# Two steps at a time in the loops of a staged attention on one Trainium2 core

## The chip, the core and the metric

The kernel runs on one core of one Trainium2 chip. The time is the device time of one execution in microseconds (us). The engines work side by side, each on an instruction list of its own, and meet only at semaphores: TensorE (PE in the profile, its weight loads are PEld), ScalarE (ACT), VectorE (DVE), GpSimd (POOL) and SyncE (SP), which here only starts transfers.

## What is computed

x is 2 batches of 1024 rows of 128 numbers. Four attentions, two linear layers and two mixtures of experts follow each other, each behind a layer norm and added to x. All attentions have 16 heads of 64 and work on 1024 queries and 1024 keys of a batch:

```python
# a0: keys and values shared by all heads, no mask
sim  = einsum('bnhk,bmk->bnhm', q, k) / sqrt(64)
o    = einsum('bnhm,bmv->bnhv', softmax(sim), v)
out  = einsum('bnhv,dhv->bnd', o, output_proj)
# a1 (own keys and values for each head), a2 (latent keys and values, shared), a3 (as a1, with biases)
masked = where(causal, -inf, einsum('bhsq,bhtq->bhst', q, k))
out    = einsum('bhst,bhtv->bhsv', softmax(masked / sqrt(dq)), v)   # then the output projection
```

## The kernel before

One program of phases runs in this order: setup, norm, a0, norm, a1, norm, a2, norm, experts, norm, a3, norm, experts, final. A phase ends with a barrier of all engines. The change is in `attention_phase`, which serves a0 to a3.

**Items and steps.** A pair of heads of one batch is an item; there are 16 items. Within an item, half s of the queries (512 each) meets blocks k of 128 keys; one such meeting is a step. Without a mask (a0) an item has NS = 16 steps. With a mask it has NS = 12: four for the first half of the queries (k = 0 to 3, all on the diagonal, of 512, 384, 256 and 128 queries) and eight for the second (k = 0 to 3 of 512 queries each, k = 4 to 7 on the diagonal of 512, 384, 256, 128). Steps of all items are numbered through by g.

**What a step is on TensorE.** Round g of the loop issues four things:

- `scores(g)` (L506, L509, L514): keys by queries of both heads, two matmuls of 64 rows that lie side by side in the upper and the lower half of the array (64*128 in the profile), then minus the row maximum (L509) and, on the diagonal, the mask (L514). The result goes to one of two score buffers of two banks.
- `chunk(g + LEAD)`, LEAD = 10 (L530, L535): the same scores in a faster type, queries by up to 512 keys, also 64*128, ten steps ahead, for their row maxima only. It has one buffer of two banks, `chunk_ps`, so each chunk waits until VectorE has taken the maxima of the one before:

```python
def chunk(c):
    if c >= 1:
        pe.wait_ge(maxed, c)
```

- `mix_step(g - LAG)`, LAG = 2 (L549): probabilities by values. The two heads lie side by side in the columns of the array (128*64), and all steps of a half add up in bank 6.
- the small matmuls that the table `when` puts at this round (`use_small`): the projections `q` and `k` (L560) and `v` (L565), `top`, which transposes the row maxima (L570), `total`, the sums of the probabilities (L574, 128*64), and `out`, the output projection (L578). All but `total` use the whole array (128*128). All of them write bank 7, and each waits until the one before has been copied out:

```python
def use_small(n, kind, i, part):
    if n >= 1:
        pe.wait_ge(small_out, n)
```

**The others.** ScalarE takes exponentials (`exps`, L609), copies the finished product out of bank 6 (`take_mixed`, L617) and all small results but `out` out of bank 7 (`take_small`, L631 to L650). VectorE takes the maxima of a chunk (`row_max`, L680; L687 joins two halves), inverts the sums in four quarters (`invert`, L700), multiplies (`normalise`, L708) and adds `out` (`add_out`, L713). GpSimd adds up probabilities (`add_up`, L765) and rounds q and k (L755). Every engine's list follows the same loop over g, written out when the program is built. In an item of the masked attentions, by step number within the item, `q` stands at 9 and 0, `out` at 1 and 10, `top` at 2 and 6, `total` at 3 and 7, and in a1 and a3 also `v` at 4 and 5, `k` at 8 and 11. In a0 (of 16) `q` stands at 1 and 4, `out` at 2 and 10, `total` at 3 and 11, `top` at 6 and 14. Inversions stand at the four steps behind a `total`, the normalisation at the fifth.

Of the kernel before, what the change touches and what calls it, by code (L numbers as in the profile page):

```python
# [43 lines left out]
LEAD = 10  # L44
LAG = 2
# [337 lines left out]
def attention_phase(nc, m, a, tag, dram, after, causal, biased=False, shared=False):  # L383
# [5 lines left out]
    with phase(nc) as (ctx, new_sem):  # L389
# [33 lines left out]
        def step(g):  # L423
            i, j = divmod(g, NS)
            s, k = steps[j]
            return i, s, k, max(0, k - s * TPG) * P if causal else 0
# [28 lines left out]
            uses_at.setdefault(g, []).append((n, kind, i, part))  # L455
        FIRST = uses[0][0]
        LAST = uses[-1][0] + 1

        rounds = [(kind, i, part) for _, kind, i, part in uses if kind in "qk"]
        round_of = {one: n for n, one in enumerate(rounds)}  # L460
# [35 lines left out]
        def _(pe):  # L496
            def scores(g):
                i, s, k, lo = step(g)
                if g >= 2:
                    pe.wait_ge(exped, g - 1)  # L500
                if g == first_step(i, s):
                    pe.wait_ge(small_out, use_of["top", i, s] + 1)
                out, width = score[g % 2], BANK - lo
                diagonal = causal and k >= s * TPG
                for head, rows in enumerate(HEADS):
                    nc.tensor.matmul(out[:, head, 0:width], a.k[rows, key_slot(i, 3), k * P:(k + 1) * P],  # L506
                                     a.q[rows, i % 3, s * BANK + lo:(s + 1) * BANK], start=True, stop=False)
                for head, rows in enumerate(HEADS):
                    last = nc.tensor.matmul(out[:, head, 0:width], a.pick[rows, :], a.max_row[rows, s, lo:BANK],  # L509
                                            start=False, stop=not diagonal)  # L510
                if diagonal:
                    for half in range(2):
                        for head, rows in enumerate(HEADS):
                            last = nc.tensor.matmul(out[:, head, half * HD:(half + 1) * HD], a.causal[rows, half, :],  # L514
                                                    a.shifted_ident[rows, 0, 0:HD], start=False, stop=half == 1)
                last.then_inc(scored, 1)
# [64 lines left out]
            if biased:  # L581
# [3 lines left out]
                                            stop=n == PAIRS - 1)  # L585
                last.then_inc(bias_mm, 1)
                pe.wait_ge(bias_out, 1)
            for g in range(FIRST, LAST):
                if 0 <= g < TOTAL:
                    scores(g)  # L590
                if 0 <= g + LEAD < TOTAL:
                    chunk(g + LEAD)
                if 0 <= g - LAG < TOTAL:
                    mix_step(g - LAG)
                for use in uses_at.get(g, ()):
                    use_small(*use)

        @block.scalar
        def _(act):
            def exps(g):  # L600
                i, s, k, lo = step(g)
                act.wait_ge(scored, g + 1)
                if k > 0 and ring_slot[g] >= RING:
                    before = step_of_ring[ring_slot[g] - RING]
                    act.wait_ge(weighed, before + 1)
                    act.wait_ge(summed, sums_done[before])
                elif k == 0 and i > 0:
                    act.wait_ge(small_mm, use_of["total", i - 1, s] + 1)
                act.activation(probabilities(g)[:, :, lo:BANK], score[g % 2][:, :, 0:BANK - lo], ACT.Exp)\  # L609
                    .then_inc(exped, 1)  # L610

            def take_mixed(i, s):
                u = unit(i, s)
                act.wait_ge(weighed, end_step(i, s))
                if u >= 2:
                    act.wait_ge(normed, u - 1)
                act.activation(a.mixed_raw[:, u % 2, :], mix, ACT.Copy).then_inc(mixed_out, 1)  # L617

            def take_small(n, kind, i, part):
                act.wait_ge(small_mm, n + 1)  # L620
                if kind in "qk":
                    if i >= 3 and not (shared and kind == "k"):
                        act.wait_ge(scored, (i - 2) * NS)
                    slot = key_slot(i, 3) if kind == "k" else i % 3
                    dst = (a.k if kind == "k" else a.q)[:, slot, part * BANK:(part + 1) * BANK]
                    scale = SCALE if kind == "q" else 1.0
                    if biased:
                        at = 1 if kind == "k" else 0
                        if n == 0:
                            act.wait_ge(bias_scaled, 1)  # L630
                        last = act.activation(dst, small, ACT.Identity, bias=a.qk_bias[:, i // B, at:at + 1],  # L631
                                              scale=scale)
                    else:
                        last = act.activation(dst, small, ACT.Copy, scale=scale)  # L634
                elif kind == "v":
                    if shared:
                        last = act.activation(a.v[:, i, :, 0:HD], small.rearrange("p (t c) -> p t c", c=HD), ACT.Copy)
                    else:
                        if i >= 2:
                            act.wait_ge(weighed, (i - 1) * NS)  # L640
                        last = act.activation(a.v[:, i % 2, part * TPG:(part + 1) * TPG, :],
                                              small.rearrange("p (t c) -> p t c", c=P), ACT.Copy)
                elif kind == "top":
                    if i >= 1:
                        act.wait_ge(scored, end_step(i - 1, part))
                    last = act.activation(a.max_row[:, part, :], small, ACT.Copy)  # L646
                else:
                    if unit(i, part) >= 1:
                        act.wait_ge(inverted, QUARTERS * unit(i, part))
                    last = act.activation(a.total[:], small, ACT.Copy)  # L650
                last.then_inc(small_out, 1)

            for g in range(FIRST, LAST):
                if 0 <= g < TOTAL:
                    exps(g)
                if 0 <= g - LAG < TOTAL:
                    i, s, _, _ = step(g - LAG)
                    if g - LAG + 1 == end_step(i, s):
                        take_mixed(i, s)
                for n, kind, i, part in uses_at.get(g, ()):  # L660
                    if kind != "out":
                        take_small(n, kind, i, part)

        @block.vector
        def _(dve):
# [61 lines left out]
            for i in range(ITEMS):  # L727
                for s in range(2):
# [1 line left out]
                    for quarter in range(QUARTERS):  # L730
                        inverts_at[at + quarter] = (i, s, quarter)
                    norms_at[at + QUARTERS] = (i, s)
            for g in range(FIRST, LAST):
                if 0 <= g + LEAD < TOTAL:
                    row_max(g + LEAD)
                if g in norms_at:
                    normalise(*norms_at[g])
                if g in inverts_at:
                    invert(*inverts_at[g])
                for n, kind, i, part in uses_at.get(g, ()):  # L740
                    if kind == "out":
                        add_out(n, i, part)

        @block.gpsimd
        def _(pool):
            def round_off(n, kind, i, part):
                pool.wait_ge(small_out, n + 1)
                if i >= 2 and not (shared and kind == "k"):
                    pool.wait_ge(chunked, (i - 1) * NS)
                cols = slice(part * BANK, (part + 1) * BANK)  # L750
                if kind == "k":
                    src, dst = a.k[:, key_slot(i, 3), cols], a.k_near[:, key_slot(i, 2), cols]
                else:
                    src, dst = a.q[:, i % 3, cols], a.q_near[:, i % 2, cols]
                pool.tensor_copy(dst, src).then_inc(rounded, 1)  # L755

            def add_up(g):
                i, s, k, lo = step(g)
                pool.wait_ge(exped, g + 1)
                if k == 1:  # L760
                    pool.wait_ge(weighed, g)
                else:
                    pool.wait_ge(summed, sums_done[g] - 1)
                sums = a.sums[:, unit(i, s) % 2, :, lo:BANK]
                pool.tensor_tensor(sums, sums, probabilities(g)[:, :, lo:BANK], ALU.add).then_inc(summed, 1)  # L765

            for g in range(FIRST, LAST):
                if 0 <= g - 1 < TOTAL and step(g - 1)[2] > 0:
                    add_up(g - 1)
                for n, kind, i, part in uses_at.get(g, ()):  # L770
                    if kind in "qk":
                        round_off(n, kind, i, part)
# [308 lines left out]
```

## Time and profile before

| | us |
|---|---|
| time, median of 3 runs | 3050.87 (3048.06 to 3052.62) |
| time of the profiled execution | 3052.27 |
| its span, first to last instruction | 3050.4 |
| TensorE busy | 2823.4 (93%) |
| VectorE busy | 1749.3 (57%) |
| GpSimd busy | 1479.3 (48%) |
| ScalarE busy | 1196.1 (39%) |

The profile takes one execution; busy time is a mean over phases with different limits. In a row of TensorE the start is when the instruction began and the duration runs to the moment when its last column has left the array, so rows of matmuls that follow each other overlap: what one costs is read from its start to the start of the next.

### The profile page before, as it was taken

The numbers are of one execution on the slowest core, as the hardware profiler recorded it, in microseconds if no ns is written. First come the engines' busy times: TensorE is split into PE (matmuls) and PEld (weight loads), VectorE is DVE, ScalarE is ACT, GpSimd is POOL, SyncE is SP. The second block draws the span as 40 slices with busy tenths as digits, with TensorE's granted clock in tenths as the row PEclk, the third lists the DMA queues.
The fourth block names the chain that finished last, engine by engine and source line by source line (L and its number), as shares of the span: only waits on it lengthen the run. The fifth ranks groups of instructions, "written<-read, shape, count | busy, mean of one in ns | idle before, by whom it ended". The sixth has DMA issues, their size and how long they took to land. (4 is left out here: it accounts for less than half of the span.)

```text
span 3050.4 us, 41067 instructions
## 1 busy us (share of the span) xinstructions
PE 2823.4 (93%) x16065; PEld 1207.0 (40%) x16065; DVE 1749.3 (57%) x2337; ACT 1196.1 (39%) x1607; POOL 1479.3 (48%) x932
## 2 busy tenths in 40 slices
PE   4999999999949999999948999999787999999978
PEld 3333333333324444444423444444333444444433
DVE  2566666666573555555573666666543555555653
ACT  2344444444413444444412444444222444444422
POOL 1576677766703555555502555555301555555520
PEclk9999999999958999999956999999897999999979
DMA  4000000000000000000001000000000000000000
GB/s 101 1 1 1 1 1 1 1 1 1 1 1 16 1 1 1 1 1 1 1 0 28 1 1 1 1 1 1 1 0 1 1 1 1 1 1 1 1 1 14
DMA packets 21345, 14.63 MB, mean 5 GB/s; under 512 B 3233, under 2 KB 20001, under 8 KB 21026
## 3 DMA queue, kind: packets, MB, share of 16 engines
q1 hardware_dynamic: 21154, 12.01, 1.6%
q8 instruction: 128, 2.10, 0.3%
q14 instruction: 63, 0.52, 0.1%
HBM read 9.91 MB, written 2.10 MB: 4 GB/s over the span
## 5 line engine op out<-in xcount | busy, mean ns | idle before, releaser
L765 POOL TENSOR_TENSOR sums<-sums,p 128x1024 f32<-128x1024 f32 (+3 forms) x704 | 1352.0, 1920 | 696.6 <-PE ps L549 626.4
L680 DVE TENSOR_REDUCE half_max<-ps 128x2 f32<-128x1024 f32 (+3 forms) x640 | 703.4, 1099 | 665.0 <-PE ps L530 537.5
L609 ACT ACTIVATE p<-ps 128x1024 f32<-128x1024 f32 (+3 forms) x704 | 597.6, 849 | 666.8 <-PE ps L509 384.1
L506 PE MATMUL ps<-q,k 64*128 64x512 f32 (+3 forms) x3328 | 819.0, 569 | 0.0
L549 PE MATMUL ps<-p,v 128*64 128x512 f32 (+3 forms) x2816 | 635.0, 530 | 0.0
L509 PE MATMUL ps<-max_row,pick 64*128 64x512 f32 (+3 forms) x1664 | 572.2, 681 | 0.0
L700 DVE RECIPROCAL inverse<-total 128x128 f32<-128x128 f32 x512 | 478.8, 940 | 51.2 <-ACT total L650 40.8
L506 PEld LDWEIGHTS ps<-q,k 64*128 64x128 f32 x3328 | 251.3, 185 | 509.0 <-issue 340.4
L530 PE MATMUL ps<-k_near,q_near 64*128 64x512 f32 (+2 forms) x1664 | 340.7, 403 | 27.9 <-DVE half_max L680 21.4
L680 DVE TENSOR_REDUCE neg_max<-ps 128x2 f32<-128x256 f32 x192 | 158.5, 826 | 331.0 <-PE ps L535 330.7
L755 POOL CAST k_near<-k 128x512 fp32r<-128x512 f32 x72 | 44.0, 611 | 464.4 <-ACT k L634 261.7
L530 PEld LDWEIGHTS ps<-k_near,q_near 64*128 64x128 f32 x1664 | 164.1, 191 | 153.1 <-issue 107.5
L509 PEld LDWEIGHTS ps<-max_row,pick 64*128 64x128 f32 x1664 | 161.7, 188 | 143.6 <-issue 129.0
L755 POOL CAST q_near<-q 128x512 fp32r<-128x512 f32 x128 | 78.2, 611 | 287.7 <-ACT q L634 242.7
L549 PEld LDWEIGHTS ps<-p,v 128*64 128x64 f32 x2816 | 139.9, 134 | 156.5 <-issue 122.5
L609 ACT ACTIVATE sums<-ps 128x1024 f32<-128x1024 f32 x128 | 131.0, 1023 | 145.4 <-PE ps L509 85.0
L578 PE MATMUL ps<-mixed,o_w 128*128 128x512 f32 x256 | 147.7, 659 | 24.3 <-DVE mixed L708 24.3
L560 PE MATMUL ps<-xn_t,q_w 128*128 128x512 f32 x256 | 154.3, 686 | 5.7 <-ACT k L634 2.7
L650 ACT ACTIVATE total<-ps 128x512 f32<-128x512 f32 x128 | 76.4, 597 | 169.7 <-PE ps L574 169.7
L549 PE MATMUL ps<-sums,v 128*64 128x512 f32 x512 | 138.1, 617 | 0.1
L574 PE MATMUL ps<-sums,ones 128*64 128x512 f32 x512 | 132.6, 596 | 4.1 <-DVE y_t L713 2.3
L646 ACT ACTIVATE max_row<-ps 128x512 fp32r<-128x512 f32 x128 | 76.4, 597 | 151.2 <-PE ps L570 151.2
(138 smaller groups left out, 2067.4 us busy)
## 6 DMA issues: line engine op xcount, KB each, us to landing
q_w<-in_wq SPq DMA_DIRECT2D x3, 512.0 KB
o_w<-in_wo SPq DMA_DIRECT2D x3, 512.0 KB
k_w<-in_wk SPq DMA_DIRECT2D x2, 512.0 KB
v_w<-in_wv SPq DMA_DIRECT2D x2, 512.0 KB
out<-x SPq DMA_DIRECT2D x4, 256.0 KB, 2.8
scratch<-in_wq_t SPq DMA_DIRECT2D x1, 512.0 KB, 5.1
scratch<-in_w_out SPq DMA_DIRECT2D x1, 512.0 KB, 7.2
wq_latent<-scratch SPq DMA_DIRECT2D x1, 512.0 KB, 3.3
```

The source lines that it names most:

```text
L506: nc.tensor.matmul(out[:, head, 0:width], a.k[rows, key_slot(i, 3), k * P:(k + 1) * P], a.q[rows, i % 3, s * BANK + lo:(s + 1) * BANK], st ...
L509: last = nc.tensor.matmul(out[:, head, 0:width], a.pick[rows, :], a.max_row[rows, s, lo:BANK], start=False, stop=not diagonal)
L530: last = nc.tensor.matmul(chunk_ps[:, head, 0:hi - lo], a.q_near[rows, i % 2, t * P:(t + 1) * P], a.k_near[rows, key_slot(i, 2), lo:hi], s ...
L549: last = nc.tensor.matmul(mix[rows, lo:BANK], a.v[:, key_slot(i, 2), k, value_columns(head)], probabilities(g)[:, head, lo:BANK], start=k ...
L560: last = nc.tensor.matmul(small, weights, m.xn_t[:, at:at + BANK], start=True, stop=True)
L574: last = nc.tensor.matmul(small[rows, :], a.ones[:], a.sums[:, unit(i, part) % 2, head, :], start=True, stop=True)
L578: last = nc.tensor.matmul(small, w.o[:, i // B, :], a.mixed[:], start=True, stop=True)
L609: act.activation(probabilities(g)[:, :, lo:BANK], score[g % 2][:, :, 0:BANK - lo], ACT.Exp)\
L680: last = v.tensor_reduce(out, chunk_ps[:, :, 0:hi - lo], AX.X, ALU.max, negate=True)
L700: v.reciprocal(a.inverse[:, cols], a.total[:, cols]).then_inc(inverted, 1)
L755: pool.tensor_copy(dst, src).then_inc(rounded, 1)
L765: pool.tensor_tensor(sums, sums, probabilities(g)[:, :, lo:BANK], ALU.add).then_inc(summed, 1)
```

## The change

On TensorE, ScalarE and VectorE the loop takes two steps, g and g + 1 with g even: first scores (or exponentials, or maxima) of both, then both products (or what belongs to them), then the small matmuls of both (or their copies, or additions). GpSimd's order stays. No instruction and no wait is added or removed.

```diff
+        PAIRS_OF_STEPS = [(g, g + 1) for g in range(FIRST - FIRST % 2, LAST, 2)]
...
-            for g in range(FIRST, LAST):
-                if 0 <= g < TOTAL:
-                    scores(g)
-                if 0 <= g + LEAD < TOTAL:
-                    chunk(g + LEAD)
-                if 0 <= g - LAG < TOTAL:
-                    mix_step(g - LAG)
-                for use in uses_at.get(g, ()):
-                    use_small(*use)
+            for pair in PAIRS_OF_STEPS:
+                for g in pair:
+                    if 0 <= g < TOTAL:
+                        scores(g)
+                    if 0 <= g + LEAD < TOTAL:
+                        chunk(g + LEAD)
+                for g in pair:
+                    if 0 <= g - LAG < TOTAL:
+                        mix_step(g - LAG)
+                for g in pair:
+                    for use in uses_at.get(g, ()):
+                        use_small(*use)
...
+                for g in pair:
+                    if 0 <= g + LEAD < TOTAL:
+                        row_max(g + LEAD)
+                for g in pair:
+                    if g in norms_at:
+                        normalise(*norms_at[g])
+                    if g in inverts_at:
+                        invert(*inverts_at[g])
+                for g in pair:
+                    for n, kind, i, part in uses_at.get(g, ()):
+                        if kind == "out":
+                            add_out(n, i, part)
```

ScalarE's loop is changed in the same way: `exps` of both, `take_mixed`, `take_small` of both.

TensorE in a1, steps 6 and 7 of an item, before (a name left of the arrow is written, names right of it are read; x2 and x4 count equal matmuls):

```order
L506 MATMUL ps<-q,k 128x512 x2
L509 MATMUL ps<-max_row,pick 128x512 x2
L530 MATMUL ps<-k_near,q_near 128x512 x2
L549 MATMUL ps<-sums,v 64x512 x2
L570 MATMUL ps<-ident,neg_max 128x128 x4
L506 MATMUL ps<-q,k 128x512 x2
L509 MATMUL ps<-max_row,pick 128x512 x2
L530 MATMUL ps<-k_near,q_near 128x128 x2
L535 MATMUL ps<-causal,shifted_ident 128x128 x4
L549 MATMUL ps<-p,v 64x512 x2
L574 MATMUL ps<-sums,ones 64x512 x2
```

The same two steps after the change, where lines of TensorE's code are one higher:

```order
L507 MATMUL ps<-q,k 128x512 x2
L510 MATMUL ps<-max_row,pick 128x512 x2
L531 MATMUL ps<-k_near,q_near 128x512 x2
L507 MATMUL ps<-q,k 128x512 x2
L510 MATMUL ps<-max_row,pick 128x512 x2
L531 MATMUL ps<-k_near,q_near 128x128 x2
L536 MATMUL ps<-causal,shifted_ident 128x128 x4
L550 MATMUL ps<-sums,v 64x512 x2
L550 MATMUL ps<-p,v 64x512 x2
L571 MATMUL ps<-ident,neg_max 128x128 x4
L575 MATMUL ps<-sums,ones 64x512 x2
```

Both pairs of scores and chunk now stand ahead of both products, and `total` (L575) stands straight behind `top` (L571), where two scores, a chunk and a product stood between them.

VectorE in a1, steps 10 and 11, before:

```order
L680 TENSOR_REDUCE half_max<-ps 128x2
L700 RECIPROCAL inverse<-total 128x128
L680 TENSOR_REDUCE half_max<-ps 128x2
L700 RECIPROCAL inverse<-total 128x128
L713 TENSOR_TENSOR y_t<-y_t,ps 128x512
```

After, where L680 is L687, L700 is L707 and L713 is L720:

```order
L687 TENSOR_REDUCE half_max<-ps 128x2 x2
L707 RECIPROCAL inverse<-total 128x128 x2
L720 TENSOR_TENSOR y_t<-y_t,ps 128x512
```

The second maximum has moved ahead of an inversion and of the addition of `out`, and the addition now stands behind both inversions.

## Rows read from the trace of the kernel before

**Rows 1.** The page, busy time of the engines.

```profile
PE 2823.4 (93%) x16065; PEld 1207.0 (40%) x16065; DVE 1749.3 (57%) x2337; ACT 1196.1 (39%) x1607; POOL 1479.3 (48%) x932
```

**Rows 2.** Windows, a steady item of a0 and of a1: stretch, length, each engine's busy us, clock.

```profile
200.00:247.66 47.66, 47.66 (x220) 16.78 (x216) 29.92 (x31) 21.15 (x24) 34.23 (x17) 1.00 0.00 1
1200.00:1237.58 37.58, 37.58 (x258) 16.85 (x254) 21.77 (x25) 16.75 (x25) 19.36 (x14) 1.00 0.01 1
```

**Rows 3.** Timeline of TensorE in a0: start, us, engine, line, operation, names, form, count.

```profile
402.13 1.08 PE L549 MATMUL ps<-sums,v 128*64 128x512 f32 x4
403.14 1.12 PE L578 MATMUL ps<-mixed,o_w 128*128 128x512 f32 x2
404.20 1.13 PE L506 MATMUL ps<-q,k 64*128 64x512 f32 x4
...
405.73 1.08 PE L549 MATMUL ps<-p,v 128*64 128x512 f32 x4
406.63 1.03 PE L574 MATMUL ps<-sums,ones 128*64 128x512 f32 x4
407.59 0.70 PE L506 MATMUL ps<-q,k 64*128 64x512 f32 x2
```

**Rows 4.** Timeline of TensorE, start of a1: chunks that waited; in brackets idle time before.

```profile
942.16 0.49 PE L530 MATMUL ps<-k_near,q_near 64*128 64x512 f32 x2
943.98 0.45 PE L530 MATMUL ps<-k_near,q_near 64*128 64x384 f32 x2 [1.32 <-DVE half_max L680]
...
944.48 0.70 PE L560 MATMUL ps<-xn_t,k_w 128*128 128x512 f32 x1
...
951.20 0.33 PE L530 MATMUL ps<-k_near,q_near 64*128 64x128 f32 x2 [0.64 <-DVE half_max L680]
...
951.58 0.65 PE L549 MATMUL ps<-sums,v 128*64 128x512 f32 x2
```

**Rows 5.** The same start of a1, VectorE.

```profile
942.70 1.23 DVE L680 TENSOR_REDUCE half_max<-ps 128x2 f32<-128x1024 f32 x1 [1.62 <-PE ps L530]
```

**Rows 6.** Groups by line and form, VectorE's maxima: busy us, mean ns, idle before.

```profile
L680 DVE TENSOR_REDUCE half_max<-ps 128x2 f32<-128x1024 f32 x496 | 605.1, 1220 | 599.8 <-PE ps L530 537.5 <-PE ps L535 62.0
...
L680 DVE TENSOR_REDUCE neg_max<-ps 128x2 f32<-128x768 f32 x48 | 46.0, 959 | 115.4 <-PE ps L535 115.4
L680 DVE TENSOR_REDUCE neg_max<-ps 128x2 f32<-128x256 f32 x48 | 20.4, 426 | 61.3 <-PE ps L535 61.0
```

**Rows 7.** Timeline of TensorE, steady a1: steps 11, 2 (its transposes) and 3.

```profile
1202.54 0.49 PE L506 MATMUL ps<-q,k 64*128 64x128 f32 x4
...
1203.49 0.54 PE L549 MATMUL ps<-p,v 128*64 128x384 f32 x2
...
1213.73 0.66 PE L570 MATMUL ps<-ident,neg_max 128*128 128x128 f32 x4
1214.32 0.49 PE L506 MATMUL ps<-q,k 64*128 64x128 f32 x4
...
1215.20 0.54 PE L549 MATMUL ps<-p,v 128*64 128x384 f32 x2
```

**Rows 8.** Timeline of TensorE, end of a3: two small matmuls in a row.

```profile
2928.76 1.10 PE L578 MATMUL ps<-mixed,o_w 128*128 128x512 f32 x2 [1.53 <-DVE mixed L708]
2930.63 1.08 PE L574 MATMUL ps<-sums,ones 128*64 128x512 f32 x4 [0.78 <-DVE y_t L713]
```

**Rows 9.** The same end of a3, VectorE.

```profile
2929.89 0.69 DVE L713 TENSOR_TENSOR y_t<-y_t,ps 128x512 f32<-128x512 f32 x1 [1.28 <-PE ps L578]
```

**Rows 10.** Groups by line and form: an inversion, ScalarE's copy of `total`.

```profile
L700 DVE RECIPROCAL inverse<-total 128x128 f32<-128x128 f32 x512 | 478.8, 940 | 51.2 <-ACT total L650 40.8
...
L650 ACT ACTIVATE total<-ps 128x512 f32<-128x512 f32 x128 | 76.4, 597 | 169.7 <-PE ps L574 169.7
```

**Rows 11.** Windows at the start of a3: as rows 2; 1.00 or 0.50 is the clock.

```profile
2331.20:2334.60 3.40, 2.18 (x16) 1.19 (x14) 2.16 (x3) 0.60 (x1) 0.00 (x0) 1.00 0.00 0
2334.60:2338.00 3.40, 3.37 (x10) 0.95 (x8) 1.40 (x2) 0.69 (x1) 0.61 (x1) 0.50 0.00 0
```

More of the change, by code:

```diff
@@ L651, in take_small @@
                 last.then_inc(small_out, 1)
[L653 to L662, printed above, removed]
+            for pair in PAIRS_OF_STEPS:
+                for g in pair:
+                    if 0 <= g < TOTAL:
+                        exps(g)
+                for g in pair:
+                    if 0 <= g - LAG < TOTAL:
+                        i, s, _, _ = step(g - LAG)
+                        if g - LAG + 1 == end_step(i, s):
+                            take_mixed(i, s)
+                for g in pair:
+                    for n, kind, i, part in uses_at.get(g, ()):
+                        if kind != "out":
+                            take_small(n, kind, i, part)
         @block.vector
@@ L732, in _ @@
                     norms_at[at + QUARTERS] = (i, s)
[L733 to L742, printed above, removed]
+            for pair in PAIRS_OF_STEPS:
+                for g in pair:
+                    if 0 <= g + LEAD < TOTAL:
+                        row_max(g + LEAD)
+                for g in pair:
+                    if g in norms_at:
+                        normalise(*norms_at[g])
+                    if g in inverts_at:
+                        invert(*inverts_at[g])
+                for g in pair:
+                    for n, kind, i, part in uses_at.get(g, ()):
+                        if kind == "out":
+                            add_out(n, i, part)
         @block.gpsimd
@@ L765, in add_up @@
                 pool.tensor_tensor(sums, sums, probabilities(g)[:, :, lo:BANK], ALU.add).then_inc(summed, 1)
-            for g in range(FIRST, LAST):
+            for g in range(PAIRS_OF_STEPS[0][0], PAIRS_OF_STEPS[-1][-1] + 1):
                 if 0 <= g - 1 < TOTAL and step(g - 1)[2] > 0:
```

## The prediction, made before the changed kernel was run

> **What bounds the kernel now.** First the page: TensorE is busy 93% of the span, the next engine 57% [rows 1]. That share is a mean, so then windows over one steady item: 47.66 us in a0 and 37.58 in a1, TensorE busy in all of them, no gap, clock 1.00 [rows 2]; The 16 items of these two make 763 and 601 us; a2 and a3 go through the same code as a1. In the attentions, then, whatever lengthens TensorE's list lengthens the kernel, and everything else is hidden. So the question is what each piece costs from its start to the next start, and which waits of TensorE are satisfied only because other work stands between.
>
> **What the change can save.** Before, TensorE goes scores, product, small, scores. A product between two pieces of another shape takes 1.01 us (402.13 to 403.14); followed by `total`, which has the product's shape (128*64), 0.90 (405.73 to 406.63) [rows 3]. Leaving a shape thus costs 0.11; `total` itself leaves the shape but does not enter it and takes 0.96 (406.63 to 407.59), so the bare work of such matmuls is 0.85, and entering a shape costs 0.05. Two products in a row save 0.16 a pair; where one of them had `total` behind it, which now stands behind `top` or `out`, only 0.05. Scores behind a chunk save a similar amount, below. The Trainium skill, "TensorEngine Tiling (Array Packing)", Key Properties, says that a change of tiling mode drains TensorE. The trace agrees, at 0.11 for the drain, and by this rule alone the kernel gets faster (rival 2).
>
> **Wait 1: the second chunk.** Chunk c + 1 waits for the maxima of chunk c. Before, the next scores, a product and perhaps a small matmul covered them; now only `scores(g + 1)` does. The start of a1 shows the wait bare: chunk at 942.16 ends 942.65, maxima 942.70 to 943.93, next chunk 943.98 [rows 4, 5], so 0.05 on either side. Maxima take 1.22, 0.96 and 0.43 us for chunks of 512, 384 and 128 keys [rows 6]. A chunk's end lies 0.07 behind the start of the next piece (403.21 against 403.14) [rows 3]. Behind a wait a chunk takes 0.50 with 384 keys and mask, 0.38 with 128 [rows 4], so 0.56 and 0.44 for 512 and 256, and 0.42 for 512 without mask (0.49 less 0.07) [rows 4]. Hence the second scores and chunk of a pair now take 0.17 + maxima + chunk instead of their length of before.
>
> - a0: before 1.53 (404.20 to 405.73) [rows 3]; now 0.17 + 1.22 + 0.42 = 1.81. +0.28 a pair, 8 pairs: +2.2 an item.
> - Masked: before, the six odd steps take 1.54, 0.88, 1.65, 1.48, 1.42, 0.95, together 7.92 (step 11 from 1202.54 to 1203.49, step 3 from 1214.32 to 1215.20; two of the six) [rows 7]. Now 6 x 0.17 = 1.02, maxima of the first chunks 4 x 1.22 + 0.96 + 0.43 = 6.27, second chunks 2 x 0.56 + 2 x 0.44 + 0.38 + 0.50 = 2.88: 10.17. +2.25 an item. The worst pair is steps 10 and 11, whose second scores are 128 wide: +0.94.
>
> This contains what the missing change of shape saves. Products give back 6 x 0.16 + 2 x 0.05 = 1.06 in a0, 4 x 0.16 + 2 x 0.05 = 0.74 in a masked item.
>
> **Wait 2: two small matmuls in one pair.** Both write bank 7, and the second waits until ScalarE or VectorE has copied out the first. Before, scores, a chunk and a product stood between, 0.88 us for scores and chunk alone at the narrowest pair (step 3) [rows 7]. Now nothing does. By the table, one item has such doubles at steps (2,3) and (10,11) in a0; (0,1), (2,3), (6,7) in a2; at all six pairs in a1 and a3. The end of a3 shows one: `out` starts 2928.76, ends after 1.10, VectorE adds 0.69 from 2929.89, `total` starts 2930.63, so 1.87 start to start [rows 8, 9]; without the wait it is 1.06 (403.14 to 404.20) [rows 3]. The follower costs 1.08 instead of 1.03 [rows 3, 8], so 0.05 more. With ScalarE's copy (0.60) [rows 10]:
>
> - 512-column matmuls: 1.12 + 0.05 + 0.60 + 0.05 = 1.82, then 1.11; before 2 x 1.06. +0.81.
> - `top`, `total`: transposes end after 0.66 (before they took 0.59, 1213.73 to 1214.32) [rows 7]: 0.66 + 0.70 + 1.01 against 0.59 + 0.96. +0.82.
> - `out`, `total` in a0: 1.87 + 1.01 against 2.02. +0.86.
> - `out`, `k` (steps 10 and 11): VectorE first has the second maxima, 0.96, and two inversions of 0.94 [rows 6, 10], together some 2.8 us behind the chunk; the matmul ends at about 2.7, so it costs 0.1 more. +0.95.
>
> Sums an item: a0 1.7, a2 2.45, a1 5 x 0.82 + 0.95 = 5.05, a3 the same (its copies add a bias, which I take to cost nothing).
>
> **VectorE later.** Both maxima now stand ahead of inversions, normalisation and addition. Behind the second maxima, 1.27 us after the chunk, two inversions are done at 3.1. In a0 the next chunk ends no earlier than 1.86 + 1.53 = 3.39: covered, by 0.3. In a1 and a3 small matmuls cover it. In a2 steps 2 to 5 have no small matmul between: two narrow products (0.8) and scores (1.53) end at 2.3, so maxima start 0.7 late: +0.7 an item there. If cover in a0 is gone too, four pairs lose up to 0.3 each, +20 us in all; from below it is nothing. ScalarE and GpSimd have time: 21.15 and 34.23 of 47.66 us [rows 2].
>
> **The sum.** a0: 2.2 - 1.06 + 1.7 = 2.9; a1 and a3: 2.25 - 0.74 + 5.05 = 6.55; a2: 2.25 - 0.74 + 2.45 + 0.7 = 4.7. Times 16 items: 46 + 105 + 105 + 75 = 331. The first item of each attention has uses ahead of step 0 that already stood bare, about half an item of each: 10 less, 321. The profiled execution took 3052.3, with a span of 3050.4, and becomes 3373; it lies 1.4 above the median of the runs, so 3372 by the median. **Forecast 3373.**
>
> **Rivals.**
>
> 1. *The clock falls.* At the start of a3 a stretch of 3.4 us with TensorE busy 2.18 was followed by one at clock 0.50 [rows 11]. The new order puts up to two waits of nearly 1 us close together (steps 0 and 1: maxima, then `q`, `out`), with busy shares by the profile's count near two thirds. Against it: the rest of each item is dense, and by the terms above TensorE waits in under a fifth of it. If each of 48 masked items lost one such stretch, half of 3.4 us, it costs 48 x 1.7 = 82: **3455**; twice an item 3540. The Trainium skill, "TensorE: Matmul & The Clock Gate", section on psum-queue depth-cycling, describes such oscillation from short idle times between groups.
> 2. *The other side: no wait decides, only changes of shape go.* 416 pairs save 0.16 on products and, by the same size, on scores: 0.3 x 416 = 125, so **2926**. It needs the maxima to be back in time: in a0 their round trip is 0.05 + 1.22 + 0.05, the scores that cover it are under 1.2 long (1.53 less chunk and drain), so it decides from a maximum of about 1.0 us, and needs wait 2 to vanish as well. Nothing in the trace speaks for that.
> 3. *Only wait 1 counts*, since something covers bank 7: 331 less 16 x (1.7 + 5.05 + 5.05 + 2.45) = 228 leaves 103: **3155**. The end of a3 speaks against it.
> 4. *The change does nothing*, as every wait was in force already: excluded by windows without a gap [rows 2].
>
> **How the numbers follow.** Forecast 0.68, between 3310 and 3430: terms taken singly may be off by 0.1 a wait, 27 us over the 272 doubles and 42 over the 416 pairs. Rival 1 0.16, rival 2 0.05, rival 3 0.10, rival 4 0.01. The range goes from 3290 to 3460 and holds the forecast and half of rival 1. A measurement can tell 0.2% from no change, 6 us; faster 0.05, same 0.01, slower 0.94.
>
> **What the profile after would show.** A steady item of 50.6 us in a0, 44.1 in a1, 38.0 in a2 (from 33.3, an estimate: 37.58 less two `k` at 1.06 and two `v` that I take for 1.1), 44.1 in a3, clock 1.00. The chunk's line waits for VectorE's maxima about 416 times, some 0.3 to 1.1 us each; bank 7's lines (L561, L566, L575, L579) wait for ScalarE or VectorE about 270 times, 0.75 us each. Products in a row cost 0.85 each but for the ends. Wrong would be: an item of a0 under 47.66 (rival 2), no idle time ahead of the second small matmul (rival 3), or stretches at clock 0.50 within the attentions (rival 1).

## The result, and the profile after

| | before | after |
|---|---|---|
| median of 4 runs, us | 3049.89 | 3418.6 (3417.54 to 3423.54) |
| span of the profiled execution, us | 3050.4 | 3421.5 |

The ratio is 1.121, 95% interval 1.119 to 1.123: 369 us slower. The forecast was 3373, its range 3290 to 3460.

The page of the kernel after, engines' busy time and the granted clock in 40 slices:

```profile
span 3421.5 us, 41067 instructions
...
PE 2824.4 (83%) x16065; PEld 1263.3 (37%) x16065; DVE 1735.7 (51%) x2337; ACT 1203.4 (35%) x1607; POOL 1476.1 (43%) x932
...
PEclk9999999999958999999967999999886999999988
```

TensorE does the same work in the same busy time (2824.4 against 2823.4 [rows 1]), but it is spread over 371 us more. Windows over one steady item each of a0, a1, a2 and a3, columns as in [rows 2]:

```profile
404.33:457.84 53.51, 47.51 (x218) 18.19 (x216) 30.45 (x31) 21.18 (x24) 34.16 (x16) 1.00 0.00 1
1200.00:1243.85 43.85, 37.50 (x258) 17.41 (x254) 21.18 (x25) 16.91 (x25) 19.29 (x15) 1.00 0.00 1
2000.00:2037.93 37.93, 32.99 (x234) 14.94 (x232) 21.04 (x25) 14.51 (x20) 18.47 (x12) 1.00 0.00 1
2700.00:2744.05 44.05, 37.49 (x252) 17.40 (x252) 21.17 (x26) 17.26 (x24) 19.29 (x14) 1.00 0.00 1
```

Where TensorE was busy for the whole item before, it now rests 6.0 us of 53.5 in a0 and 6.35 of 43.85 in a1, at clock 1.00. In the view of waits (who waited, for whom: us in total, times, longest) the rows of before for the chunk and bank 7 came to little:

```profile
PE ps L530 <- DVE half_max L680: 21.4, 22, 1.4
...
PE ps L560 <- ACT k L634: 5.5, 8, 0.7
```

After the change they are among TensorE's longest:

```profile
PE ps L531 <- DVE half_max L687: 170.3, 322, 1.4
...
PE ps L575 <- ACT max_row L650: 61.8, 90, 0.7
...
PE ps L507 <- ACT max_row L650: 27.1, 35, 0.8
...
PE ps L575 <- DVE y_t L720: 25.0, 32, 0.8
```

The first row is the second chunk waiting for the maxima of the first. L575 is `total`, waiting in bank 7 for the copy of `top` or the addition of `out`; with the rows of L561, L566 and L579, which wait for other copies and for that addition, bank 7 comes to 188 us in 261 waits. L507 are scores that wait for a copy of transposed maxima: that row was in no term of the forecast. Steps 10 and 11 of a1, TensorE after the change, then VectorE:

```profile
1207.63 0.70 PE L507 MATMUL ps<-q,k 64*128 64x256 f32 x4
...
1208.36 0.48 PE L531 MATMUL ps<-k_near,q_near 64*128 64x512 f32 x2
1208.67 0.39 PE L507 MATMUL ps<-q,k 64*128 64x128 f32 x4
...
1210.15 0.44 PE L531 MATMUL ps<-k_near,q_near 64*128 64x384 f32 x2 [0.95 <-DVE half_max L687]
...
1210.65 1.72 PE L550 MATMUL ps<-p,v 128*64 128x512 f32 x8
1212.31 1.13 PE L579 MATMUL ps<-mixed,o_w 128*128 128x512 f32 x2
1214.22 1.12 PE L561 MATMUL ps<-xn_t,k_w 128*128 128x512 f32 x2 [0.78 <-DVE y_t L720]
1215.27 1.13 PE L507 MATMUL ps<-q,k 64*128 64x512 f32 x4
```

```profile
1208.87 1.22 DVE L687 TENSOR_REDUCE half_max<-ps 128x2 f32<-128x1024 f32 x1 [2.71 <-PE ps L531]
1210.77 0.96 DVE L687 TENSOR_REDUCE half_max<-ps 128x2 f32<-128x768 f32 x1 [0.67 <-PE ps L536]
1211.64 1.75 DVE L707 RECIPROCAL inverse<-total 128x128 f32<-128x128 f32 x2
1213.47 0.69 DVE L720 TENSOR_TENSOR y_t<-y_t,ps 128x512 f32<-128x512 f32 x1
```

Both forecast waits stand here with their releasers: the chunk at 1210.15 follows the maxima that end at 1210.09, and `k` at 1214.22 follows the addition that ends at 1214.16. The two products (1210.65 to 1212.31) take 1.66 us where they took 1.01 and 0.80 before: a saving of 0.15, as forecast (0.16).

### The profile page after: what moved, and what is told of

It reads as the page before. It is cut to its first block and busy times, and to the rows that moved or that the text cites. A ratio compares the mean times of both kernels' runs of the same rounds, so it can differ in the third digit from the quotient of the medians.

```text
span 3421.5 us, 41067 instructions
## 1 busy us (share of the span) xinstructions
PE 2824.4 (83%) x16065; PEld 1263.3 (37%) x16065; DVE 1735.7 (51%) x2337; ACT 1203.4 (35%) x1607; POOL 1476.1 (43%) x932
## 5 line engine op out<-in xcount | busy, mean ns | idle before, releaser
L687 DVE TENSOR_REDUCE half_max<-ps 128x2 f32<-128x1024 f32 (+3 forms) x640 | 705.0, 1101 | 927.8 <-PE ps L531 802.4
L507 PE MATMUL ps<-q,k 64*128 64x512 f32 (+3 forms) x3328 | 786.3, 548 | 27.1 <-ACT max_row L650 27.1
L550 PE MATMUL ps<-p,v 128*64 128x512 f32 (+3 forms) x2816 | 566.4, 515 | 0.0
L531 PE MATMUL ps<-k_near,q_near 64*128 64x512 f32 (+2 forms) x1664 | 369.4, 438 | 184.0 <-DVE half_max L687 170.3
L707 DVE RECIPROCAL inverse<-total 128x128 f32<-128x128 f32 x512 | 448.6, 920 | 57.3 <-ACT total L654 43.7
L507 PEld LDWEIGHTS ps<-q,k 64*128 64x128 f32 x3328 | 282.8, 187 | 324.9 <-issue 297.7
L687 DVE TENSOR_REDUCE neg_max<-ps 128x2 f32<-128x256 f32 x192 | 158.6, 826 | 350.6 <-PE ps L536 350.6
L550 PEld LDWEIGHTS ps<-p,v 128*64 128x64 f32 x2816 | 176.5, 136 | 244.4 <-issue 169.2
L575 PE MATMUL ps<-sums,ones 128*64 128x512 f32 x512 | 140.8, 629 | 90.6 <-ACT max_row L650 61.8
L579 PE MATMUL ps<-mixed,o_w 128*128 128x512 f32 x256 | 151.2, 674 | 60.6 <-DVE mixed L715 31.1
L561 PE MATMUL ps<-xn_t,q_w 128*128 128x512 f32 x256 | 154.5, 687 | 27.7 <-ACT k L635 13.2
L720 DVE TENSOR_TENSOR y_t<-y_t,ps 128x512 f32<-128x512 f32 x128 | 88.0, 688 | 162.4 <-PE ps L579 159.2
```

The costliest lines, as they stand in the source:

```text
L531: last = nc.tensor.matmul(chunk_ps[:, head, 0:hi - lo], a.q_near[rows, i % 2, t * P:(t + 1) * P], a.k_near[rows, key_slot(i, 2), lo:hi], s ...
L550: last = nc.tensor.matmul(mix[rows, lo:BANK], a.v[:, key_slot(i, 2), k, value_columns(head)], probabilities(g)[:, head, lo:BANK], start=k ...
L561: last = nc.tensor.matmul(small, weights, m.xn_t[:, at:at + BANK], start=True, stop=True)
L575: last = nc.tensor.matmul(small[rows, :], a.ones[:], a.sums[:, unit(i, part) % 2, head, :], start=True, stop=True)
L579: last = nc.tensor.matmul(small, w.o[:, i // B, :], a.mixed[:], start=True, stop=True)
L687: last = v.tensor_reduce(out, chunk_ps[:, :, 0:hi - lo], AX.X, ALU.max, negate=True)
```

## Experiments

All times are medians; "before" was run beside each group and had 3047.9, 3049.5 and 3047.4 us.

**e1, small matmuls apart.** The even step's small matmul stands ahead of both products, the odd one's behind them, and the copies on ScalarE and VectorE follow.

```diff
+                for use in uses_at.get(pair[0], ()):
+                    use_small(*use)
                 for g in pair:
                     if 0 <= g - LAG < TOTAL:
                         mix_step(g - LAG)
-                for g in pair:
-                    for use in uses_at.get(g, ()):
-                        use_small(*use)
+                for use in uses_at.get(pair[1], ()):
+                    use_small(*use)
...
```

> The changed order, but the small matmul of the even step stands between scores and products, that of the odd step behind the products, so bank 7 is copied out under two products. Theory (two waits, each with its own price): wait 2 goes, and with it the wait of a0's scores for the copy of the transposes; left are the wait of the second chunk for its maxima and VectorE's lateness: a0 49.8 us an item, a1 and a3 38.9, a2 35.3, the whole about 3155. Rival (one common cause, such as VectorE or ScalarE late behind both maxima): most of the loss stays, over 3300.

Measured: 3216.1 us, 1.054 of before (1.053 to 1.056), 203 us under the changed kernel. Items: 49.4, 39.4, 36.4, 39.4 us. Bank 7's waits are gone from the list of waits, but for a few that the kernel before has too, and the chunk's stay nearly as they were:

```profile
PE ps L531 <- DVE half_max L692: 175.4, 322, 2.5
...
PE ps L579 <- DVE mixed L720: 52.5, 52, 4.9
```

So wait 2 and its kin carry 203 of 369 us. The rest is larger than expected by 61: 27 us in the items, where L579 (`out`) now waits 52 times for the normalisation (11 times and 31.1 us in the changed kernel), and the remainder outside the steady items.

**e2, chunks apart.** Both scores stand between the two chunks.

```diff
+                for c in (pair[0] + LEAD,):
+                    if 0 <= c < TOTAL:
+                        chunk(c)
                 for g in pair:
                     if 0 <= g < TOTAL:
                         scores(g)
-                    if 0 <= g + LEAD < TOTAL:
-                        chunk(g + LEAD)
+                for c in (pair[1] + LEAD,):
+                    if 0 <= c < TOTAL:
+                        chunk(c)
```

> The changed order, but with both scores between the two chunks (chunk, scores, scores, chunk, product, product, both small). Theory: wait 1 goes but for the narrow scores of steps 10 and 11, wait 2 stays: about 220 us under the changed kernel, 3200. Rival (the second chunk's wait only hides another one behind it): less than 100 us under the changed kernel.

Measured: 3261.0 us, 1.070 (1.068 to 1.071), 158 us under the changed kernel. Items: 50.1 to 52.0 in a0 (median 50.9), then 41.0, 35.8, 41.1. The chunk's waits fall from 170.3 us in 322 to 77.3 us in 98:

```profile
PE ps L531 <- DVE half_max L691: 77.3, 98, 1.8
...
PE ps L575 <- ACT max_row L654: 61.8, 90, 0.7
```

Wait 1 is a cause of its own, and the row of `total` behind `top` is the same to 0.1 us. Not all of the gain is wait 1's: in a0 a chunk now stands between `top` and the scores that wait for its copy, and that row (L507) falls from 27.1 to 10.6 us. The gain is still less than the expected 220: fewer waits, but longer ones, are left. In a0 one chunk an item waits 1.75 us, because VectorE's join of two halves of maxima (L698) takes 2.05 us in place of 0.17; e5 and e7 below show why. TensorE, VectorE, and a window behind that wait (columns as in [rows 11]):

```profile
435.28 0.50 PE L531 MATMUL ps<-k_near,q_near 64*128 64x512 f32 x2 [1.76 <-DVE half_max L691]
```

```profile
430.43 2.05 DVE L698 TENSOR_TENSOR neg_max<-half_max 128x8 f32<-128x8 f32 x1
```

```profile
436.00:439.40 3.40, 3.40 (x10) 0.82 (x7) 2.72 (x3) 0.00 (x0) 3.26 (x2) 0.50 0.00 0
```

Behind nine of these fifteen waits the clock fell to 0.50 for 3.4 us. Items with such a stretch take about 1.7 us more (51.73 against 50.05), so the clock costs e2 some 15 us, an estimate from these items.

**e3, both apart.** The edits of e1 and e2 together.

> Both repairs at once; two steps still go together, so the saved changes of shape stay (0.16 us on products and 0.15 on scores of a pair). Theory: about 2945, 3.5% under the kernel before. Rival (changes of shape cost nothing in themselves, the drain only moves): within 0.5% of the kernel before, 3050.

Measured: 3104.2 us, 1.018 (1.017 to 1.020). Neither theory: items of a0 46.9 and of a1 and a3 37.25 are shorter than before (47.66, 37.58), so changes of shape do cost time in themselves; but a2's take 35.3 or, in most cases, 36.9 instead of 33.3. Something that neither repair touches was left. In a2, TensorE's one long wait, then VectorE and GpSimd ahead of it:

```profile
1852.48 0.44 PE L531 MATMUL ps<-k_near,q_near 64*128 64x384 f32 x2 [2.04 <-DVE half_max L696]
```

```profile
1846.67 2.81 DVE L724 TENSOR_TENSOR mixed<-mixed_raw,inverse 128x512 f32<-128x512 f32 x1
1849.58 1.76 DVE L716 RECIPROCAL inverse<-total 128x128 f32<-128x128 f32 x2
1851.26 1.16 DVE L696 TENSOR_REDUCE half_max<-ps 128x2 f32<-128x1024 f32 x1
```

```profile
1846.58 2.35 POOL L786 TENSOR_TENSOR sums<-sums,p 128x1024 f32<-128x1024 f32 x1
```

The normalisation takes 2.81 us; elsewhere the same one takes 0.69. It began 0.09 after an addition on GpSimd, and it ends 0.55 after that addition does. The maxima behind it are late by as much. Behind this wait the clock fell too (columns as in [rows 11]), as it did nine times in a2. The items of 35.3 us are those without such a stretch, so the late maxima cost a2 2.0 us an item and the clock 1.6 more where it fell:

```profile
1853.80:1857.20 3.40, 3.40 (x9) 0.76 (x8) 2.61 (x4) 0.00 (x0) 2.21 (x3) 0.50 0.00 0
```

**e4, the transposes first.** In a0 alone `top` stands ahead of the products, and its copy on ScalarE ahead of `take_mixed`.

```diff
+        def early(use):
+            return not causal and use[1] == "top"
...
+                for g in pair:
+                    for use in uses_at.get(g, ()):
+                        if early(use):
+                            use_small(*use)
                 for g in pair:
                     if 0 <= g - LAG < TOTAL:
                         mix_step(g - LAG)
...
```

> The changed kernel, but in a0 alone the transposes of the maxima stand ahead of the two products of their pair instead of behind them. Theory (the scores of the next half waited 0.85 us for ScalarE's copy of the transposes, twice an item): 16 x 1.7 = 27 us under the changed kernel, 3391, item of a0 51.8. Rival (that wait would be replaced by VectorE's lateness): under 10 us.

Measured: 3391.7 us, 1.112 (1.110 to 1.114), 27 us under the changed kernel; an item of a0 51.8. Both as expected. The wait it removes, in a0 of the changed kernel:

```profile
431.64 0.66 PE L571 MATMUL ps<-ident,neg_max 128*128 128x128 f32 x4
433.08 1.09 PE L507 MATMUL ps<-q,k 64*128 64x512 f32 x3 [0.78 <-ACT max_row L650]
...
436.42 0.65 PE L550 MATMUL ps<-p,v 128*64 128x512 f32 x2
```

1.44 us from start to start, where the transposes took 0.59 before [rows 7].

**e5, short additions.** GpSimd adds one column per head and leaves out the others, so the sums are not the real ones; every wait stays.

```diff
-                sums = a.sums[:, unit(i, s) % 2, :, lo:BANK]
-                pool.tensor_tensor(sums, sums, probabilities(g)[:, :, lo:BANK], ALU.add).then_inc(summed, 1)
+                sums = a.sums[:, unit(i, s) % 2, :, lo:lo + 1]
+                pool.tensor_tensor(sums, sums, probabilities(g)[:, :, lo:lo + 1], ALU.add).then_inc(summed, 1)
```

> The changed kernel, but GpSimd adds one column of each head instead of all, so the sums are not the real ones; every semaphore stays. Theory (the short join of two halves of maxima, 0.17 us alone but 1.56 beside GpSimd, waits until GpSimd's running addition ends, and makes the next maxima late once an item of a0): the join takes 0.17 everywhere, an item of a0 52.5 instead of 53.5 us, the whole some 20 us under the changed kernel. Rival (VectorE is late by its own queue alone): within 5 us of the changed kernel.

Measured: 3398.4 us, 1.114 (1.113 to 1.116), 20 us under the changed kernel; an item of a0 52.5. Groups by line and form, busy us and mean ns, first of the changed kernel, then of e5:

```profile
L715 DVE TENSOR_TENSOR mixed<-mixed_raw,inverse 128x512 f32<-128x512 f32 x128 | 95.3, 744 | 0.9 <-PE ps L561 0.6
...
L694 DVE TENSOR_TENSOR neg_max<-half_max 128x8 f32<-128x8 f32 x80 | 35.4, 442 | 8.0
```

```profile
L715 DVE TENSOR_TENSOR mixed<-mixed_raw,inverse 128x512 f32<-128x512 f32 x128 | 87.9, 687 | 1.0 <-PE ps L561 0.6
...
L694 DVE TENSOR_TENSOR neg_max<-half_max 128x8 f32<-128x8 f32 x80 | 13.9, 173 | 8.0
```

**e6, both apart and short additions.** The edits of e3 and e5.

> Both repairs (chunks apart, small matmuls apart) and the one-column additions. Theory (what the repaired order still loses is VectorE's join and normalisation held up by GpSimd): waits for the maxima, 24 us in a0, 20 in a1, 47 in a2, shrink to a quarter, item of a2 near 33.3 instead of 36.9, the whole about 3010. Rival (VectorE's list is too long between two chunks whatever GpSimd does): within 20 us of 3104.

Measured: 2998.3 us, 0.983 (0.982 to 0.985), 106 us under e3. An item of a2 takes 33.5 instead of 36.9, one of a0 44.95, one of a1 36.5. This kernel leaves out work of GpSimd, so it is no version to use; it shows that what e3 lost, it lost through GpSimd's additions. That GpSimd itself was late can explain little of it, for TensorE waited 7.6 us in all for its sums in e3 (L575 for L786). What is left is VectorE held up beside the additions, and the falls of the clock behind the long waits, some 15 us of the 106 (nine stretches in a2, 1.6 to 1.7 us each).

**e7, the join with one input.** e3, GpSimd's work in full, and only the form of one small operation changed.

```diff
-                        v.tensor_tensor(a.neg_max[:, s, :, 0:P:HD], a.half_max[:, 0], a.half_max[:, 1], ALU.min)\
-                            .then_inc(max_ready, 1)
+                        v.tensor_reduce(a.neg_max[:, s, :, 0:P:HD], a.half_max[:].rearrange("p a t h -> p t h a"),
+                                        AX.X, ALU.min).then_inc(max_ready, 1)
```

> Both repairs, and the join of the maxima written as a reduction that reads one tensor, with GpSimd's additions in full. Theory (an operation with two inputs in on-chip memory waits for GpSimd, one with one input does not): the join takes under 0.3 us beside GpSimd too, a0's one wait of 1.3 to 1.5 us an item goes, the whole some 30 to 40 us under 3104. Rival (any short operation is held up): no change.

Measured: 3075.1 us, 1.009 (1.007 to 1.010), 29 us under e3, at the lower edge of what was expected. The same groups of e7:

```profile
L724 DVE TENSOR_TENSOR mixed<-mixed_raw,inverse 128x512 f32<-128x512 f32 x128 | 218.4, 1706 | 1.0 <-issue 0.6
...
L703 DVE TENSOR_REDUCE neg_max<-half_max 128x8 f32<-128x16 f32 x80 | 13.8, 173 | 8.5
```

The join takes 173 ns in all 80 cases beside full additions; in e3 it took 718 in the mean. The normalisation, with two inputs still, takes 1706. An item of a0 takes 44.95 as in e6, and TensorE waits nowhere in it. Items of a1, a2 and a3 are as in e3, and in a2 the clock still falls.

**e8, where it pays.** e7, but a2 and the rounds ahead of step 0 go singly. Of the edit, the list of pairs:

```diff
+        if shared and causal:
+            PAIRS_OF_STEPS = [(g,) for g in range(FIRST, LAST)]
+        else:
+            PAIRS_OF_STEPS = [(g,) for g in range(FIRST, 0)] + [(g, g + 1) for g in range(0, LAST, 2)]
...
```

> Both repairs and the one-input join, but a2, whose list leaves VectorE the least cover, and the rounds ahead of step 0 everywhere go one step at a time as before. Theory: a2 takes its 523 us of before, the starts theirs, a0 and a1 gain 0.8 and 0.3 to 0.8 us an item: 3015 to 3030, under the kernel before. Rival (starts and clock cost more than the items gain): 3050 or above.

Measured: 3012.6 us, 0.988 of before (0.986 to 0.989), 37 us faster than the kernel before. I had expected 3015 to 3030, 2 us more at the least. Items: 44.95, 37.25, 33.3, 37.25.

**e9, starts singly.** The changed kernel, with pairs from step 0 on only (the second branch of e8's edit for all attentions).

> The changed kernel, but the rounds ahead of step 0 of each attention go one at a time as before. Theory (outside the steady items the change also costs some 29 us: in the starts two small matmuls and two chunks in a row wait bare, and the clock rises later): 20 to 30 us under the changed kernel, steady items unchanged. Rival (the starts wait for copies in either order): within 5 us.

Measured: 3395.9 us, 1.115 (1.113 to 1.117), 23 us under the changed kernel, items unchanged at 53.5, 43.85, 37.9 and 44.05.

**e10, both omissions of a0 taken away.** The changed kernel with the edit of e4 and e7's join.

> The changed kernel with the two things that the forecast left out of a0 taken away together: transposes ahead of the products in a0, and the join of the maxima reading one tensor. Theory: they add up to the whole miss, so an item of a0 takes 50.8 us (forecast 50.6) and the whole 27 + 20 us less than the changed kernel, about 3373. Rival (they overlap): only the larger of the two, 3391.

Measured: 3377.9 us, 1.109 (1.107 to 1.110), an item of a0 50.8 us, as expected; the whole 5 above the expected 3373. In the item the two add up (1.7 and 1.0 of 2.7); in the whole they give 41 us together, and 27 and 20 singly.

## Why the prediction was right, and where it missed

The direction, the two waits and most of the sum held; the time came out 46 us above the forecast. Items, from one transposition of row maxima to the same one an item on:

| item of | before | forecast | measured | with e10 |
|---|---|---|---|---|
| a0 | 47.66 | 50.6 | 53.5 | 50.8 |
| a1 | 37.58 | 44.1 | 43.85 | 43.85 |
| a2 | 33.3 | 38.0 | 37.9 | 37.9 |
| a3 | 37.58 | 44.1 | 44.05 | 44.05 |

**What the change can save: right.** The forecast had 0.16 us a pair on products and a similar amount on scores. With all waits out of the way, an item of a0 in e7 takes 44.95 instead of 47.66, 2.7 for 8 pairs, 0.34 a pair. Rival 2, that only this would count, fell: in a0 the saving was there in full, under waits that were larger. The page "TensorEngine Tiling (Array Packing)" of the Trainium skill, Key Properties, says that a change of tiling mode drains TensorE; this number agrees, for fewer changes of mode took less time. In the masked attentions as much is not shown: even in e6 an item of a1 gained 1.05 us for 6 pairs, and one of a2 lost 0.2, with some waits of 0.3 to 0.5 us left in them.

**Wait 1, the second chunk: right.** In a0 a pair's scores and chunks should take 1.53 + 1.81 = 3.34; from 433.08 to the products at 436.42 (e4's rows) they took 3.34. The two halves are not as I had split them: the second scores start 1.40 after the first, not 1.53, and the products 1.94 after those, not 1.81. The change of shape saved ahead of the second scores only moves them nearer to the chunk whose maxima are waited for, so the sum stays. The worst pair, steps 10 and 11 of a1, was forecast at +0.94; it takes 3.02 (1207.63 to 1210.65) against 1.14 and 0.95 before, +0.93. Of the 416 waits forecast the list shows 332 (322 for `half_max`, 10 for `neg_max`), those of a0 with 0.23 us idle each.

**Wait 2, bank 7: right, one size slightly off.** A double of 512-column matmuls costs 1.81 and then 1.05, not 1.82 and 1.11. Here `q` and `out` in a2, with the next scores at 2034.96:

```profile
2032.10 1.13 PE L561 MATMUL ps<-xn_t,q_w 128*128 128x512 f32 x2
2033.91 1.12 PE L579 MATMUL ps<-mixed,o_w 128*128 128x512 f32 x2 [0.69 <-ACT q L638]
```

So the follower's extra 0.05, which I took from `total` [rows 3, 8], holds for `total` alone. And `out` with `k` costs 1.91 and 1.05, +0.85 instead of +0.95. Together these explain the 0.25 by which a1 came out under its forecast. An item of a3 takes 0.2 more than one of a1, as I had put the bias in its copies at nothing; the copy of `q` without and with a bias, busy us and mean ns:

```profile
L638 ACT ACTIVATE q<-ps 128x512 f32<-128x512 f32 x96 | 57.5, 599 | 139.9 <-PE ps L561 139.9
...
L635 ACT ACTIVATE q<-ps,qk_bias 128x512 f32<-128x512 f32 x32 | 22.0, 687 | 31.1 <-PE ps L561 31.1
```

Two such copies an item are waited for, 0.09 each. Rival 3 fell with e1: 203 us went with wait 2 and the scores' wait for `top`.

**VectorE later: right in a2, mis-sized in a0.** In a2 the item came to 37.9 as forecast, and by the cause named: in the pair behind the narrow products (steps 6 and 7) the first chunk ends at 2008.85, its maxima start at 2009.68, behind two inversions, and the second chunk waits 0.97 us. In a0 I wrote "covered, by 0.3" and allowed 20 us in all. One of the two joins of an item took 1.56 us instead of 0.17, and the chunk behind it waited 1.25:

```profile
451.19 1.56 DVE L694 TENSOR_TENSOR neg_max<-half_max 128x8 f32<-128x8 f32 x1
452.67 1.75 DVE L707 RECIPROCAL inverse<-total 128x128 f32<-128x128 f32 x2
```

```profile
455.55 0.50 PE L531 MATMUL ps<-k_near,q_near 64*128 64x512 f32 x2 [1.25 <-DVE half_max L687]
```

The term of the sum behind this is the cover in a0, set to nothing; it measured 1.0 us an item, 14 to 20 in all (e10 against e4, and e5). "ScalarE and GpSimd have time" was true and beside the point: GpSimd was not late, it kept VectorE out.

**Missing from wait 2: the first scores of a half.** They wait for the copy of `top`. In the masked attentions `total` stands behind `top` and has paid for that wait already; in a0 nothing does. I listed doubles by the table and did not ask who else waits for a copy in bank 7. Twice 0.85 us an item, 27 us in all (e4).

**The starts and ends: mis-sized.** I took 10 us off the sum because the first items lose less. Between their first and last scores the four attentions grew by 86, 93, 69 and 94 us, 342 together, which is 30 less than 16 whole items each (372). But another 29 lie outside, in the starts and the phases between, where I had nothing. In a1 the first projection lies 30.0 us before the first scores in the kernel before (915.5 to 945.5) and 37.3 after (1006.5 to 1043.8); windows over both stretches:

```profile
915.50:945.50 30.00, 24.01 (x82) 10.57 (x82) 10.28 (x11) 5.37 (x9) 3.68 (x6) 0.62 0.14 39
```

```profile
1006.50:1043.80 37.30, 27.42 (x82) 11.82 (x82) 10.34 (x11) 5.37 (x9) 3.68 (x6) 0.50 0.11 31
```

The same 82 matmuls and weight loads, but the clock stays at 0.50 for the whole start. TensorE's busy time takes 3.4 of the 7.3 us more and its idle time 3.9; no run separates the clock from the waits here. With single steps (e9) the same stretch takes 27.9 us at a mean clock of 0.69, and the whole 23 us less. The sum closes: 16 items of each attention were forecast at 331 and measure 372, of which a0 has 47 too much and a1, a2 and a3 together 6 too few; starts and ends were forecast at -10 and measure -30 + 29 = -1. That makes 371, the growth of the span.

**Rival 1, the clock: small in the changed kernel.** There it fell to 0.50 within an attention only twice, for 3.4 us each near the ends of a1 and a2, although TensorE waited 322 times for `half_max`, up to 1.4 us, and 261 times at bank 7, up to 0.8 us. With one longer wait an item it fell again and again: nine times in e3's a2 (2.04 us) and nine times in e2's a0 (1.75 us), not behind each of them. The page "TensorE: Matmul & The Clock Gate" of the Trainium skill, on psum-queue depth-cycling, describes a kernel in which frequent short idle times of TensorE between groups of matmuls make the clock swing between its two levels. The trace agrees in that idle time of TensorE came ahead of the falls (rows at 1853.80 and 436.00 above). It differs in the kind: one long wait an item came ahead of them, while in the changed kernel many short ones left the clock up.

## What to carry to other kernels

Putting two steps together saves changes of shape, but it also takes away the work that stood between a producer and its reader. Before such a change, list for every buffer with one slot what stands between two uses of it, in time, and compare that with the round trip of its reader; then ask for each copy who else waits for it. Here the better pair was chunk, scores, scores, chunk, small, products, small, the same grouping by shape with the covers kept: 1.8% slower than before instead of 12% (e3). It took two more steps to come out 1.2% faster (e8): VectorE's join in a form that GpSimd does not hold up, and single steps in a2 and at the starts, where pairs did not pay.

## What the runs showed of the hardware

A VectorE operation with two inputs in on-chip memory does not run beside a GpSimd addition: it ends 0.033 us (the join) or 0.55 us (the normalisation) after the addition that was running when it came, which is its own length less 0.14. It holds for every join and normalisation that began beside such an addition: 92 in the kernel before (77 of them longer by it), 63 after (21) and 107 in e3 (all), each within 0.02 us. Maxima and additions from TensorE's banks, and inversions, with at most one such input, kept their 1.22, 0.69 and 0.94 us beside GpSimd. In the changed kernel one such case, VectorE's join and the GpSimd addition it fell into:

```profile
450.37 2.35 POOL L775 TENSOR_TENSOR sums<-sums,p 128x1024 f32<-128x1024 f32 x1
```

It ends at 452.72, the join at 452.75. The page "SBUF — State Buffer" of the Trainium skill states this for a VectorE instruction with two SBUF inputs against a GpSimd instruction that reads SBUF. Writing the join as a reduction over one tensor took it out of the rule (e7); for the normalisation no run changed the form. I had read past it in the kernel before, where the join already took 0.31 us in the mean with 0.17 as its least, hidden by slack:

```profile
L687 DVE TENSOR_TENSOR neg_max<-half_max 128x8 f32<-128x8 f32 x80 | 24.9, 311 | 8.7 <-PE ps L578 0.9
```
